# Two turns through the tensor engine moved by one unit in a three-stage attention and expert kernel

## Chip, cores and metric

The kernel runs on 1 core of a Trainium2 chip. The metric is the device time of one execution in microseconds. The kernel before the change took 1273.53 us (median of three runs, 1271.52 to 1274.54).

## What is computed

Two layers over tokens `x` of 4 batches x 512 positions x 256 channels, in float32. Cut to what matters here:

```
x = x + L0_xattn(layernorm(x), ctx, ctx, mask)     # 16 heads of 16 channels, masked softmax
x = x + L0_ffn(layernorm(x))                        # self-attention, then 8 experts, the best one is used
x = x + L1_xattn(layernorm(x), ctx, ctx)            # cross-attention again, no mask
x = x + L1_ffn(layernorm(x))                        # 8 experts, the best one is used

# each attention, per batch and head:
scores = q @ k.T / 4                                # 512 x 512
scores = where(mask == 0, -inf, scores)             # first attention only
out    = softmax(scores) @ v                        # then one projection by W_O for all heads
```

## The kernel before

The program is one sequence of stages on one core: attention `xa0` (cross, masked), attention `sa0` (self), the experts `me0`, attention `xa1` (cross, no mask), the experts `me1`. Every engine has its own instruction list, written out by hand in Python, and semaphores tie them together. What runs first on an engine is the order in which the Python writes it; nothing reorders the work.

An attention stage first projects q, k and v for all batches, splits q and k into bf16 parts and parks them in DRAM. Then `attend_*` does the softmax. Its work is cut so:

- A **batch** has four **groups** of four heads. There are 4 batches, so 16 groups G = 0 to 15 in a stage; g is the group's place in its batch.
- A group has 16 **units** u = 0 to 15: key tile u // 4 (128 keys) and head u % 4.
- Each head is needed twice. Once as scores with queries on partitions, of which VectorE takes the row maximum (`scores`, line 958, and `maximum`, L373 with the mask, L377 without). And once transposed, with keys on partitions, from which ScalarE makes the exponentials (`transposed_scores`, L971, with the mask added by a second product, L975, in `xa0`; `exps`, L885).
- The maxima run 28 units ahead of the exponentials (`LEAD`), since an exponential can only be taken once the maximum of its row is known. The maximum is subtracted inside the product of L971: three extra rows of q hold the negated maximum in three bf16 parts.

How the maxima get there is what the change touches. When the last maximum of a group is taken (unit 3), VectorE cuts the 512 x 4 maxima into three bf16 parts (`split`, four small operations, L1125 to L1131). TensorE **turns** them, in `attend_tensor`'s `maxima(G)`, line 993: four products of 128 x 12 by an identity, so that the result has 12 partitions. They lie in the one spare PSUM bank, `MISC`. ScalarE copies them to SBUF (`attend_scalar`'s `maxima`, L898), and the sync engine sends them by DMA (`shift`, L792) into the extra rows of q, where group G + 1 needs them from its unit 0 on.

The bank `MISC` is shared by all small turns: a user on TensorE first waits until the last one's result was read (`take_misc`). In turn they are the maxima (unit `M_STEP` = 8), the finished output of the group before (`turn`, L1016, unit `TURN_STEP` = 12), in `xa0` the turned mask of the next batch (`turn_mask`, L1005, eight transposes of 128 x 128, at `MASK_STEPS`, group 2 and group 3, unit 9; ScalarE reads each by L904), and the output projection of the batch before (L1025 in group 1, L1036 in groups 2 and 3).

The probabilities times v (`products`, L985) run per key tile, behind the units 5, 9 and 13, and for the last key tile behind unit 1 of the next group. One call is four heads, each with a 32-column stationary operand at its own 32 partitions of the output, in float32. The profile shows eight matrix products for one call.

Six PSUM banks hold the two kinds of scores, three each (`DEEP`), so the transposed scores of unit u wait for the exponentials of unit u - 3 (semaphore `p_exp`), and the scores that TensorE makes in unit u wait for the maximum that was made of the unit three before (`s_max`).

The inner loop of TensorE, cut to what decides the order:

```
for u in range(UNITS):
    transposed_scores(b, g, u, first)
    scores(s, v, ...)
    if at >= 0 and at % HG == 0:          # u = 5, 9, 13
        products(G, g, at // HG)
    if u == M_STEP and not (last and g == NG - 1):
        maxima(G + 1)
    if u == TURN_STEP and not (first and g == 0):
        turn(G - 1)
    if a.masked and not last and (g, u) in MASK_STEPS:
        turn_mask(b + 1, i)
```

ScalarE's loop tests the same two constants: behind the exponentials of unit `M_STEP` stands the copy of the maxima, and behind those of a mask step the copy of the mask.

Of the kernel before, what the change touches and what calls it, by code (L numbers as in the profile page):

```python
# [746 lines left out]
ST, SB = 0, DEEP  # L747
OB = 2 * DEEP
MISC = OB + 1
MASK_STEPS = ((2, 9), (3, 9))  # L750
KEY_TILES = 2
MASK_ROUNDS = T // KEY_TILES
NEXT_STAGE = ((3, 5), (3, 14))
# [1 line left out]
LAST_TURN, LAST_OUT = (5, 2), (3, 4)  # L755
LATE = 2

M_STEP, TURN_STEP = 8, 12
OUT_TURNS = (3, 5)
OUT_TILES = ((2, 3), (2, 4), (3, 3), (3, 4))  # L760

# [114 lines left out]
def attend_scalar(act, a, meanwhile):  # L876
# [24 lines left out]
    def mask_copy(b, i, bank=MISC):  # L901
        act.wait_ge(a.mbT_ps.sem, a.mbT_ps.at(b, i + 1))
        batch = slice(b, b + 1) if type(b) is int else bass.ds(b, 1)
        act.activation(mem.mbT[:, batch, KEY_TILES * i:KEY_TILES * (i + 1), :].rearrange("p b k n -> p (b k n)"),  # L904
                       ps[:, bank, :].bitcast(BF16), ACT.Copy).then_inc(a.mbT_ready.sem, 1)

    def oT_copy(b, c, bank=MISC):
        act.wait_ge(a.oT_ps.sem, a.oT_ps.at(b, c + 1))
        act.activation(mem.oT[:, c, :], ps[:, bank, :], ACT.Copy).then_inc(a.oT_sb.sem, 1)

    def body(b, first, last):
        for g in range(NG):
            G = NG * b + g
            for u in range(UNITS):
# [7 lines left out]
                if last and (g, u) == HALF_TURN:  # L922
                    oT_copy(b, 0, LAST_TURN[0])
                if a.masked and not last and (g, u) in MASK_STEPS:
                    mask_copy(b + 1, MASK_STEPS.index((g, u)))

# [16 lines left out]
def attend_tensor(pe, a, meanwhile):  # L943
# [76 lines left out]
    def turn_out(b, c, bank=MISC):  # L1020
        pe.wait_ge(a.quotient.sem, a.quotient.at(NG * b + (c + 1) * NG // C - 1, QUOTIENT))
        if bank == MISC:
            take_misc()
        for t in range(T):
            ins = pe.transpose(ps[:, bank, t * P:(t + 1) * P], mem.o[:, t, c * P:(c + 1) * P], mem.ident[:, :])  # L1025
        ins.then_inc(a.oT_ps.sem, 1)
        if bank == MISC:
            misc[0] = (a.oT_sb.sem, a.oT_sb.at(b, c + 1))
# [13 lines left out]
    def body(b, first, last):  # L1042
# [4 lines left out]
        for g in range(NG):  # L1047
            G = NG * b + g
            for u in range(UNITS):
# [22 lines left out]
                if last and (g, u) == HALF_TURN:  # L1072
                    turn_out(b, 0, LAST_TURN[0])
                if a.masked and not last and (g, u) in MASK_STEPS:
                    i = MASK_STEPS.index((g, u))
                    if i == 0:
# [1014 lines left out]
```

## Time and profile before

| | |
|---|---|
| median of three runs | 1273.53 us (1271.52 to 1274.54) |
| the profiled execution: its own time | 1274.43 us |
| its span in the profile | 1272.7 us |
| TensorE busy (PE) | 1131.4 us, 89% |
| VectorE busy (DVE) | 838.6 us, 66% |
| ScalarE busy (ACT) | 660.4 us, 52% |
| GpSimd busy (POOL) | 210.9 us, 17% |
| mean granted TensorE clock | 0.949 |

PE is the matrix product, PEld the weight load that goes with it and overlaps other products. In rows of the timeline the first number is the start in us from the start of the span, the second the time covered, then the engine, the line of the kernel and the operation; x4 means that four instructions are merged into the row. A matrix product is shown from its start to a modelled end, and the next one starts before that end: the distance between two starts tells how long TensorE was taken. The attention stages lie at about 60 to 340 us (`xa0`), 395 to 620 us (`sa0`) and 925 to 1165 us (`xa1`).

### The profile page before, as it was taken

What the parts mean: (1) busy time and instruction counts of PE and PEld (TensorE: products, weight loads), DVE (VectorE), ACT (ScalarE), POOL (GpSimd) and SP (SyncE); (2) the same over time, 40 slices, a digit from 0 to 9 for tenths busy, and PEclk for the clock granted to TensorE, in tenths of its full rate; (3) what the DMA queues carried; (4) which work ended last, traced back from release to release, by engine and by line L of the source; (5) the groups of instructions that cost most, each with busy time, mean ns of one, the idle gap of its engine ahead of it and who ended that gap; (6) DMA issues with size and microseconds to landing.
All of it is one profiled execution on the core that took longest, in us unless ns stands there. A gap on an engine that the chain in (4) does not pass through costs nothing. (4 is left out here: it accounts for less than half of the span.)

```text
span 1272.7 us, 17810 instructions
## 1 busy us (share of the span) xinstructions
PE 1131.4 (89%) x5693; PEld 544.0 (43%) x5722; DVE 838.6 (66%) x2112; ACT 660.4 (52%) x1341; POOL 210.9 (17%) x272
## 2 busy tenths in 40 slices
PE   7889999999997999999967999996989999998390
PEld 4423343434453223343364666664523333335370
DVE  5878777777478888888762222223888888876722
ACT  3346666666533677677722333332537767674250
POOL 4310000000143000000202222211520010102154
PEclk9989999999999899999967999998989999999795
DMA  8953321221048433543291140103873323211064
GB/s 265 309 169 93 79 57 28 81 52 26 2 154 291 103 91 90 132 97 93 72 375 33 31 161 28 27 13 102 263 241 91 90 59 89 60 37 57 25 171 144
DMA packets 100706, 139.40 MB, mean 110 GB/s; under 512 B 8452, under 2 KB 82632, under 8 KB 99208
## 3 DMA queue, kind: packets, MB, share of 16 engines
q1 hardware_dynamic: 96536, 128.03, 33.6%
q0 software_dynamic: 4080, 10.23, 2.9%
q8 instruction: 48, 0.79, 0.3%
q14 instruction: 42, 0.34, 0.1%
HBM read 86.30 MB, written 52.17 MB: 109 GB/s over the span
## 5 line engine op out<-in xcount | busy, mean ns | idle before, releaser
L885 ACT ACTIVATE r<-ps 128x512 f32<-128x512 f32 x768 | 427.4, 600 | 211.9 <-PE ps L971 122.1
L377 DVE TENSOR_REDUCE m<-ps 128x1 f32<-128x512 f32 x512 | 320.9, 682 | 45.2 <-PE ps L958 44.9
L971 PE MATMUL ps<-r 99*128 99x512 bf16 x768 | 294.3, 388 | 5.6 <-ACT r L885 5.6
L958 PE MATMUL ps<-r 96*128 96x512 bf16 x720 | 280.9, 393 | 20.5 <-DVE m L377 7.0
L373 DVE CUSTOM_DVE_ANT_0 r<-ps,r 128x512 bf16<-128x512 f32 x256 | 170.2, 690 | 60.2 <-PE ps L958 59.6
L985 PE MATMUL ps<-r 128*32 128x512 f32 x1536 | 204.9, 605 | 4.9 <-ACT r L885 3.3
L971 PEld LDWEIGHTS ps<-r 99*128 99x128 bf16 x768 | 74.4, 98 | 211.7 <-ACT r L885 157.3
L958 PEld LDWEIGHTS ps<-r 96*128 96x128 bf16 x720 | 71.3, 99 | 105.9 <-DVE m L377 24.3
L861 POOL COPY r<-r 128x256 f32<-128x256 f32 x48 | 19.0, 399 | 542.1 <-PE ps L985 542.1
L1660 DVE COPY r<-ps 128x512 f32<-128x512 f32 x46 | 31.8, 691 | 91.9 <-PE ps L1707 91.9
L1707 PE MATMUL ps<-r 128*128 x184 | 87.8, 621 | 2.7 <-issue 0.4
L1619 ACT ACTIVATE r<-ps,cols 128x128 f32<-128x128 f32 x46 | 18.5, 453 | 137.8 <-PE ps L1698 137.8
L657 PE MATMUL ps<-r,w 128*128 128x512 f32 x192 | 88.2, 596 | 0.5 <-issue 0.5
L975 PE MATMUL ps<-r,identb 128*128 128x512 bf16 x227 | 87.5, 386 | 0.0
L1732 PE MATMUL ps<-r 128*128 x368 | 83.3, 380 | 1.1 <-ACT r L1629 1.1
L1671 DVE TENSOR_TENSOR r<-ps,r 128x256 f32<-128x256 f32 x46 | 19.5, 425 | 97.0 <-PE ps L1732 68.8
L1732 PEld LDWEIGHTS ps<-r 128*128 128x128 f32 x368 | 69.9, 190 | 20.1 <-issue 11.9
L589 ACT ACTIVATE r<-ps,cols 128x512 bf16<-128x512 f32 x48 | 32.9, 686 | 86.9 <-PE ps L657 72.7
L985 PEld LDWEIGHTS ps<-r 128*32 128x32 f32 x1536 | 30.3, 108 | 84.0 <-ACT r L885 65.3
L537 POOL TENSOR_TENSOR r<-r 128x512 bf16<-128x512 f32 x48 | 55.0, 1164 | 65.5 <-ACT r L594 65.5
L644 PE MATMUL ps<-w,r 128*128 128x256 f32 x192 | 45.5, 392 | 13.6 <-DMA w<-in_wa 7.4
L1629 ACT ACTIVATE r<-ps,b1c 128x128 f32<-128x128 f32 x184 | 49.9, 382 | 12.9 <-PE ps L1715 12.8
(151 smaller groups left out, 1220.5 us busy)
## 6 DMA issues: line engine op xcount, KB each, us to landing
r<-q_parts SPq DMA_DIRECT2D x48, 384.0 KB, 5.2
r<-k_parts SPq DMA_DIRECT2D x48, 384.0 KB, 6.0
k_parts<-r SPq DMA_DIRECT2D x24, 384.0 KB, 3.3
q_parts<-r SPq DMA_DIRECT2D x24, 384.0 KB, 3.1
r<-in_w SPq DMA_DIRECT2D x16, 512.0 KB, 4.9
r<-in_w SPq DMA_DIRECT2D x8, 1024.0 KB, 14.4
k_parts<-r SPq DMA_DIRECT2D x24, 256.0 KB, 3.3
q_parts<-r SPq DMA_DIRECT2D x24, 256.0 KB, 3.1
```

Source lines behind the costliest of these rows:

```text
L373: ins = dve.tensor_tensor_reduce(mem.junk[bank], mem.ps[:, bank, :], mem.mbS[:, t, :], 1.0, FLOOR, ALU.add, ALU.max, out)
L377: ins = dve.tensor_reduce(out, mem.ps[:, bank, :], AX.X, ALU.max)
L537: pool.tensor_tensor(mem.parts[n][:, 2, :], mem.res[n % 2], mem.parts[n][:, 1, :], ALU.subtract).then_inc(a.lo.sem, 1)
L657: ins = pe.matmul(ps[:, QK_BANK + n, :], a.w[:, 0 if of_query(n) else 1, c, (n % C) * P:(n % C + 1) * P], src[:, c, :], start=(c == 0), st ...
L885: act.activation(mem.probs[:, u // HG, u % HG, :], ps[:, ST + (UNITS * g + u) % DEEP, :], ACT.Exp, scale=SCALE).then_inc(a.p_exp.sem, 1)
L958: pe.matmul(ps[:, led_bank(n), :], mem.qst[g][0:ROWS, h, t * P:(t + 1) * P], mem.kst[g][0:ROWS, h, :], start=True, stop=True).then_inc(a.s ...
L971: ins = pe.matmul(out, mem.kst[g][0:KROWS, h, kt * P:(kt + 1) * P], mem.qst[g][0:KROWS, h, :], start=True, stop=not a.masked)
L975: ins = pe.matmul(out, mem.identb[:, :], mem.mbT[:, batch, kt, :].rearrange("p b n -> p (b n)"), start=False, stop=True)
L985: ins = pe.matmul(ps[h * VW:(h + 1) * VW, OB, :], mem.vg[g % 2][:, kt, h, :], mem.probs[:, kt, h, :], start=(kt == 0), stop=(kt == T - 1))
L1629: ins = act.activation(mem.midT[:, f, :], ps[:, TM[f // 4], (f % 4) * P:(f % 4 + 1) * P], ACT.Relu, bias=mem.b1c[:, bass.ds(e * FT + f, 1)])
L1707: ins = pe.matmul(ps[:, UP[k], :], mem.xT[j % 2][:, c, :], w, start=(c == 0), stop=(c == C - 1))
L1732: ins = pe.matmul(ps[:, DOWN[j % 2], 0:D], mem.midT[:, f, :], w, start=(f == 0), stop=(f == FT - 1))
```

## The change

Two constants are raised by one. Both TensorE and ScalarE (and through a semaphore the DMA of the maxima) follow them.

```diff
-MASK_STEPS = ((2, 9), (3, 9))
+MASK_STEPS = ((2, 10), (3, 10))
...
-M_STEP, TURN_STEP = 8, 12
+M_STEP, TURN_STEP = 9, 12
```

**TensorE, unit 8 and 9 of the first group of `xa0`.** L993 is the turn of the maxima, L971, L975 and L958 are one unit's products, L985 the probabilities times v. Before:

```order
L971 MATMUL ps<-r 128x512 [waits xa0_p_exp]
L975 MATMUL ps<-r,identb 128x512
L958 MATMUL ps<-r 128x512 [waits xa0_s_max]
L993 MATMUL ps<-identb,mparts 12x128 [waits xa0_m_sb,xa0_cut]
L993 MATMUL ps<-identb,mparts 12x128 x3
L971 MATMUL ps<-r 128x512 [waits xa0_p_exp]
L975 MATMUL ps<-r,identb 128x512
L958 MATMUL ps<-r 128x512 [waits xa0_s_max]
L985 MATMUL ps<-r 32x512 [waits xa0_p_exp]
L985 MATMUL ps<-r 32x512 x3
```

Now:

```order
L971 MATMUL ps<-r 128x512 [waits xa0_p_exp]
L975 MATMUL ps<-r,identb 128x512
L958 MATMUL ps<-r 128x512 [waits xa0_s_max]
L971 MATMUL ps<-r 128x512 [waits xa0_p_exp]
L975 MATMUL ps<-r,identb 128x512
L958 MATMUL ps<-r 128x512 [waits xa0_s_max]
L985 MATMUL ps<-r 32x512 [waits xa0_p_exp]
L985 MATMUL ps<-r 32x512 x3
L993 MATMUL ps<-identb,mparts 12x128 [waits xa0_m_sb,xa0_cut]
L993 MATMUL ps<-identb,mparts 12x128 x3
L971 MATMUL ps<-r 128x512 [waits xa0_p_exp]
```

The four narrow products of the maxima (12 columns) stood between two wide ones (128 columns); they now follow the narrow ones of L985 (32 columns). The same happens in all 45 groups that turn maxima inside the loop, 15 in each stage.

**TensorE, units 9 and 10 of the third group of `xa0`,** where the first half of the next batch's mask is turned (L1005). Before:

```order
L985 MATMUL ps<-r 32x512 x3
L1005 MATMUL ps<-identb,r 128x128 [waits xa0_m_sb,xa0_mbS_ready]
L1005 MATMUL ps<-identb,r 128x128 x7
L971 MATMUL ps<-r 128x512 [waits xa0_p_exp]
L975 MATMUL ps<-r,identb 128x512
L958 MATMUL ps<-r 128x512 [waits xa0_s_max]
```

Now:

```order
L985 MATMUL ps<-r 32x512 x3
L993 MATMUL ps<-identb,mparts 12x128 [waits xa0_quotient,xa0_cut]
L993 MATMUL ps<-identb,mparts 12x128 x3
L971 MATMUL ps<-r 128x512 [waits xa0_p_exp]
L975 MATMUL ps<-r,identb 128x512
L958 MATMUL ps<-r 128x512 [waits xa0_s_max]
L1005 MATMUL ps<-identb,r 128x128 [waits xa0_m_sb,xa0_mbS_ready]
L1005 MATMUL ps<-identb,r 128x128 x7
```

Between the turn of the maxima and that of the mask there was a unit, its wide products and the products of a key tile; now there is one unit. The mask turn still waits for `m_sb`, ScalarE's copy of the maxima. This occurs six times.

## Rows read from the trace of the kernel before

**Rows 1.** Stretches `xa0`, `xa1`: busy us (and instructions) of PE, PEld, DVE, ACT, POOL; clock.

```profile
60.00:340.00 280.00, 270.37 (x1495) 104.45 (x1521) 203.55 (x648) 174.02 (x304) 13.53 (x25) 0.98 0.25 70
...
925.00:1165.00 240.00, 227.32 (x1260) 81.42 (x1258) 198.64 (x412) 160.76 (x306) 22.19 (x32) 0.98 0.32 89
```

**Rows 2.** Timeline of PE in `xa1`, units 8 to 10 of group 4.

```profile
1006.26 0.38 PE L958 MATMUL ps<-r 96*128 96x512 bf16 x1
1006.57 0.39 PE L993 MATMUL ps<-identb,mparts 128*12 128x128 bf16 x4
1006.89 0.39 PE L971 MATMUL ps<-r 99*128 99x512 bf16 x1
1007.12 0.38 PE L958 MATMUL ps<-r 96*128 96x512 bf16 x1
1007.43 1.06 PE L985 MATMUL ps<-r 128*32 128x512 f32 x8
1008.43 0.39 PE L971 MATMUL ps<-r 99*128 99x512 bf16 x1
```

**Rows 3.** Timeline of PE: a turn of 128 columns between wide products, in `xa0`.

```profile
105.40 0.38 PE L958 MATMUL ps<-r 96*128 96x512 bf16 x1
105.62 0.60 PE L1016 MATMUL ps<-ident,r 128*128 128x128 f32 x4
106.06 0.38 PE L971 MATMUL ps<-r 99*128 99x512 bf16 x1
```

**Rows 4.** Duration of one instruction of L993, ns: least, median, most.

```profile
L993 PE MATMUL ps<-identb,mparts x192: 215/219/315, 68.5 to 1141.7; 128*12 128x128 bf16 x192
```

**Rows 5.** Timeline of ACT and DVE beside Rows 2.

```profile
1007.03 0.57 ACT L898 ACTIVATE mT<-ps 12x512 bf16<-12x512 bf16 x1
1008.85 0.60 ACT L885 ACTIVATE r<-ps 128x512 f32<-128x512 f32 x1 [0.77 <-PE ps L971]
...
1005.39 1.28 DVE L377 TENSOR_REDUCE m<-ps 128x1 f32<-128x512 f32 x2
1009.07 0.69 DVE L377 TENSOR_REDUCE m<-ps 128x1 f32<-128x512 f32 x1 [0.61 <-PE ps L958]
```

**Rows 6.** Timeline of `xa0`, group 2, which turns the mask: units 8 and 9.

```profile
117.09 0.69 DVE L373 CUSTOM_DVE_ANT_0 r<-ps,r 128x512 bf16<-128x512 f32 x1
117.31 0.39 PE L993 MATMUL ps<-identb,mparts 128*12 128x128 bf16 x4
117.73 0.59 ACT L898 ACTIVATE mT<-ps 12x512 bf16<-12x512 bf16 x1
118.07 0.38 PE L958 MATMUL ps<-r 96*128 96x512 bf16 x1
```

**Rows 7.** Timeline of `sa0`, group 6: units 8 and 9. Then waits of L993 in the program.

```profile
504.75 0.68 DVE L377 TENSOR_REDUCE m<-ps 128x1 f32<-128x512 f32 x1
504.98 0.38 PE L993 MATMUL ps<-identb,mparts 128*12 128x128 bf16 x4 [0.56 <-DVE w L1171]
505.52 0.38 PE L958 MATMUL ps<-r 96*128 96x512 bf16 x1
...
  DVE w L1171: 2.2, 4
```

**Rows 8.** Timeline of `xa1`, group 14: units 8 to 10, and 14 to 0 of group 15.

```profile
1141.22 1.57 ACT L885 ACTIVATE r<-ps 128x512 f32<-128x512 f32 x3 [0.72 <-PE ps L971]
1141.88 0.39 PE L971 MATMUL ps<-r 99*128 99x512 bf16 x1
1142.36 1.07 PE L985 MATMUL ps<-r 128*32 128x512 f32 x8
1143.27 0.72 SPq L792 DMA_DIRECT2D r<-mT  x1
...
1145.92 0.82 PE L971 MATMUL ps<-r 99*128 99x512 bf16 x3
```

**Rows 9.** DMA issues: size and median us from issue to landing.

```profile
cols<-in_cols SPq DMA_DIRECT2D x1, 10.0 KB, 2.0
```

## The prediction

> **What bounds the kernel now.** I read the busy times by stage first. TensorE is busy 270.4 of 280.0 us in `xa0` and 227.3 of 240.0 us in `xa1`; VectorE has 203.6 and 198.6, ScalarE 174.0 and 160.8 [rows 1]. `sa0` looks like `xa1`. So in the attention stages the time is TensorE's, and something that shortens its list shortens the kernel, unless the time saved runs into a wait.
>
> Then the timeline of TensorE around the change, and in it only the distances between starts. Two wide products (128 columns stationary, 512 streamed) follow each other after 0.22 us: L971 at 1006.89, L958 at 1007.12 [rows 2]. From a wide product to the first narrow one it takes 0.31, both into the turn of the maxima (1006.26 to 1006.57) and into the products of a key tile (1007.12 to 1007.43). From the first of the turn to the next wide product it takes 0.32 (1006.57 to 1006.89). One instruction of the turn is shown with 0.219 us [rows 4] and four of them with 0.39, so they start 0.057 us apart, and four need 0.23; the step back to wide costs the rest, 0.09 us. As a control, a turn that is wide itself (L1016) begins 0.22 behind its wide neighbour and its four instructions take 0.44, 0.11 each, with nothing on top [rows 3]. So it isn't turning that costs, but the passage between narrow and wide: 0.09 us in, 0.09 out.
>
> The Trainium skill (TensorEngine Tiling (Array Packing), Key Properties) has a rule for this: changing the tiling mode, not merely the tile, drains the engine. The trace agrees that a passage costs something, 0.09 us. By the same rule nothing is saved if 12 and 32 columns count as different modes; the page doesn't say, and the rivals below price it from rows.
>
> **The change, step by step.**
>
> *The turn itself.* Before, it costs TensorE (0.31 - 0.22) + 0.32 = 0.41 us, two passages included. Now it stands behind products that are narrow already. If narrow to narrow costs no passage, it shares the way in with L985 and leaves only once: the call of L985 takes 1.00 to the next wide product (1007.43 to 1008.43), the turn adds 4 x 0.057 = 0.23. The trace never shows 12 columns behind 32. The bounds are: no passage between them (saving 0.41 - 0.23 = 0.18, with the unrounded starts of these rows 0.19), one passage of 0.09 (saving 0.09), or out and in again (saving 0). I take no passage, because both forms show the same 0.31 on the way in and the same 0.09 on the way out: they look like one mode. **0.19 us a turn**, 45 turns, if nothing waits: 8.4 us at the very most.
>
> *Waits that eat it.* Everything of unit 9 now comes 0.41 us earlier on TensorE, until L985, and the turn is then behind it. Two partners could be late.
>
> VectorE: the scores of unit 9 wait for the maximum of unit 6. TensorE restarts 0.09 us behind VectorE's end (504.75 + 0.68 = 505.43, scores at 505.52) [rows 7]. In group 4 of `xa1` that maximum is the second of two, ends at 1005.39 + 1.28 = 1006.67, and the scores are at 1007.12 [rows 2, 5]: 0.45 of distance, 0.41 asked for, 0.09 needed, so 0.05 is lost and 0.14 left. I find this distance in the first group of a batch (4 and 8 in `sa0`, 4, 8 and 12 in `xa1`): five groups at 0.14. The other plain groups have 0.5 or more.
>
> ScalarE: in the second group of a batch (5, 9, 13 in both stages) the exponentials are later, by the copy of the turned output; there about 0.03 is lost: six groups at 0.16.
>
> `sa0`, groups 6, 7, 10 and 11: VectorE does the residual first (L1171), and TensorE waits for it in front of the turn, 2.2 us in four waits. The scores of unit 9 then wait for VectorE anyway (505.52, 0.09 behind the maximum) [rows 7]. Here the old turn lay inside a wait and was free; the new one lies behind it. **+0.23 each**, four groups.
>
> Group 14 of `sa0` and `xa1` has no scores left, and ScalarE sets the pace. The first of its three exponentials ends at 1141.82, L971 of unit 9 starts at 1141.88 (0.06 behind), so taking the turn away in front of it gains nothing [rows 8]. Behind L985 it costs 0.23, and ScalarE's copy (0.57, in steps of 0.48) then meets the exponentials of unit 10. The turn's last product would start at about 1143.4, the copy 0.25 later (as 117.31 + 0.17 to 117.73) [rows 6], the exponential at about 1144.15, where before it was at 1143.79. **+0.35 each**, two groups.
>
> *ScalarE elsewhere.* The copy falls into an idle stretch: behind the exponential of unit 9, ScalarE waits 0.77 us for L971 of unit 10 [rows 5]. It delays that exponential by about 0.15 against TensorE. The next that needs it is unit 13, three units and more on, and TensorE reaches that later than the exponential ends. Free.
>
> *The mask turn,* six times in `xa0`. Moved from behind narrow products to between wide ones, it changes no passage: L985 still leaves narrow once, eight wide turns cost the same. But it waits for ScalarE's copy of the maxima. From the turn's last start that copy ends 0.25 + 0.59 = 0.84 later and TensorE may go on at 0.90; TensorE itself arrives after 0.15 and a unit of three wide products, 0.66, at 0.81. **0.09 lost**, 0.10 left in five groups. In group 2 the mask's preparation also holds VectorE: the maximum ends at 117.78, the scores stand at 118.07, 0.29 [rows 6], so 0.20 is lost as well: about +0.10. ScalarE's mask copy comes a unit later too, before the turn of unit 12 needs the bank; by the same steps it is out of it 0.04 us in time.
>
> *The DMA of the maxima* is issued some 1.0 us later, and what the sync engine issues behind it too. In group 14 of `xa1`, the tightest, the issue moves from 1143.27 to about 1144.3; unit 0 of group 15, the third of the three, then starts at about 1146.7 (1146.37 before) [rows 8]. 2.4 us are left, where a 10 KB load lands in 2.0 [rows 9]. Free; were it as slow as the 3.1 us that the old distance allows, it would cost 0.7 in each stage's last group.
>
> **The sum.** `xa0`: 9 plain groups x -0.19, 5 x -0.10, +0.10 = -2.1. `sa0`: 5 x -0.19, 2 x -0.14, 3 x -0.16, 4 x +0.23, +0.35 = -0.4. `xa1`: 8 x -0.19, 3 x -0.14, 3 x -0.16, +0.35 = -2.1. Together **-4.6 us**. The profiled execution took 1274.43 (span 1272.7), so 1269.8; it lies 0.9 above the median of the three runs, and on that median the forecast is **1268.9 us**.
>
> **Rivals.**
>
> *One passage remains* between L985 and the turn (a drain because the tile's shape or the number type changes, float32 to bf16). Place: the start of L993 behind the second half of L985. Price: 0.095 per turn, 45 times, 4.3 us: 1273.2. For it: no row shows the pair. Against it: wide float32 to wide bf16 costs nothing (L1016 to L971, 0.11) [rows 3].
>
> *The turn goes out and in again*, as if through the wide mode: L993 would start 0.19 later than I say. Then the saving is nil, and the losses stand alone: -4.6 + 45 x 0.19 = +3.9 us, **1277.4, slower**. It decides from the point where the passage costs more than 0.10 us. For it: 12 and 32 are different column counts. Against it: within L985 the tile changes with every head, and eight instructions fit into 1.00 us.
>
> *No loss anywhere*: the waits I have counted are softer than they look. 45 x 0.19 = 8.4 us, 1265.1. Against it: L993's waits on L1171 are plain in the trace [rows 7].
>
> *The saved time is lost at the next wait* (VectorE or ScalarE bound after all), about -0.5: 1273. Against it: both are idle in front of unit 10, 0.61 and 0.77 us [rows 5], so the groups re-align on TensorE.
>
> **How the numbers follow.** 0.2%, 2.5 us, is about what a measurement of this kernel can tell from no change. Faster by over 0.2%: 0.70 for the forecast and 0.02 for no loss anywhere, 0.72. No change: 0.13 for one passage and 0.07 for the saving lost at the next wait, 0.20. Slower by over 0.2%: 0.06 for out and in again and 0.02 for a DMA that comes late and stalls every group, 0.08. The range reaches down to 1266.4, two thirds of the way to the no-loss case, and up to 1273.6, which holds the one-passage case and the saving lost at the next wait.
>
> **What would show it.** In the profile after: L993 starts about 0.9 us behind the first L985, not 1.0 or more; L971 follows 1.22 to 1.23 behind L985's start where a turn lies between; L993 never waits on L1171; groups of `xa1` last 0.14 to 0.19 us less from turn to turn, group 14 longer; the mask turn shows an idle 0.09 in front of it. Wrong would be: L993 at 1.0 or later behind L985, or shorter distances there and yet the same span.

## The result

The changed kernel takes **1293.47 us** (median of four runs, 1290.26 to 1299.86) where the kernel before took 1274.03 (1271.52 to 1274.58). The ratio is 1.0163, with a 95% interval of 1.0121 to 1.0205: 1.6% slower. The forecast was 1268.9, faster, with a range from 1266.4 to 1273.6. It was wrong in its direction.

The page of the changed kernel: busy times, then two groups of section 5 (busy us, mean ns of one, idle us in front of it and its main releaser).

```profile
span 1290.7 us, 17839 instructions
...
PE 1131.3 (88%) x5722; PEld 547.0 (42%) x5722; DVE 840.9 (65%) x2112; ACT 663.6 (51%) x1341; POOL 210.8 (16%) x272
...
L958 PE MATMUL ps<-r 96*128 96x512 bf16 x720 | 283.5, 396 | 41.8 <-DMA r<-k_parts 24.2
L971 PE MATMUL ps<-r 99*128 99x512 bf16 x768 | 295.7, 390 | 6.1 <-ACT r L885 6.1
```

The first of these groups in the page of the kernel before, and its row among the waits (us in total, times, longest us):

```profile
L958 PE MATMUL ps<-r 96*128 96x512 bf16 x720 | 280.9, 393 | 20.5 <-DVE m L377 7.0
PE ps L958 <- DMA r<-k_parts: 3.4, 8, 0.8
```

TensorE has no more work: it is busy for 1131.3 us, 1131.4 before. VectorE and ScalarE are busy 2 and 3 us longer and stay far from the span, and the mean granted clock is nearly the same (0.947, before 0.949). The span grew by 18.0 us, and one row answers for it: in front of L958, the scores that lead by 28 units, TensorE sat idle for 20.5 us before and now for 41.8, and it is a DMA that L958 waits for, the k stack of a coming group (24.2 us). The profile of before had that wait too, in eight places and with 3.4 us. So I compared where L958 waits, and found one place: unit 4 of a group, where the first scores of the group after next need that group's q and k (its **stacks**, the rows of four heads).

First, though, the turn itself. The timeline of TensorE in `xa1` of the changed kernel, units 9 and 10 of a plain group, answers to [rows 2]:

```profile
1052.67 0.38 PE L971 MATMUL ps<-r 99*128 99x512 bf16 x1
1052.89 0.38 PE L958 MATMUL ps<-r 96*128 96x512 bf16 x1
1053.20 1.07 PE L985 MATMUL ps<-r 128*32 128x512 f32 x8
1054.08 0.39 PE L993 MATMUL ps<-identb,mparts 128*12 128x128 bf16 x4
1054.40 0.39 PE L971 MATMUL ps<-r 99*128 99x512 bf16 x1
```

The turn starts 0.88 us behind L985 and the next wide product 0.32 behind the turn: 1.20 for both, where the forecast said 1.22 to 1.23 and the one-passage rival would give 1.32. The local gain is there, a little larger than forecast.

Now the other end of the chain: the sync engine's timeline in `sa0`, first of the kernel before. L792 sends the turned maxima, L1901 loads a piece of the experts' weights, L334 loads q and k of a coming group.

```profile
451.78 0.72 SPq L792 DMA_DIRECT2D r<-mT  x1
452.56 0.41 SPq L1901 DMA_DIRECT2D r<-in_w  x1
453.02 0.42 SPq L334 DMA_DIRECT2D r<-q_parts  x1
453.48 0.48 SPq L334 DMA_DIRECT2D r<-k_parts  x1
```

And the product that waits for that load, in the timeline of TensorE (unit 4 of the next group):

```profile
459.60 0.38 PE L971 MATMUL ps<-r 99*128 99x512 bf16 x1
460.25 0.39 PE L958 MATMUL ps<-r 96*128 96x512 bf16 x1 [0.27 <-DMA r<-k_parts]
```

The same in the changed kernel, first ScalarE's copy of the maxima and the sync engine:

```profile
454.82 0.59 ACT L898 ACTIVATE mT<-ps 12x512 bf16<-12x512 bf16 x1 [0.66 <-PE ps L993]
...
455.44 0.72 SPq L792 DMA_DIRECT2D r<-mT  x1
456.21 0.41 SPq L1901 DMA_DIRECT2D r<-in_w  x1
456.67 0.42 SPq L334 DMA_DIRECT2D r<-q_parts  x1
457.13 0.48 SPq L334 DMA_DIRECT2D r<-k_parts  x1
```

and TensorE:

```profile
461.73 0.38 PE L971 MATMUL ps<-r 99*128 99x512 bf16 x1
463.70 0.39 PE L958 MATMUL ps<-r 96*128 96x512 bf16 x1 [1.58 <-DMA r<-k_parts]
```

Three things can be read here. First, the loads of the stacks stand behind L792 on the sync engine, which waits for ScalarE's copy. Second, unit 8 of this group began at 450.19 before and at 452.55 now, so the stacks are issued 2.8 us behind it before (453.02) and 4.1 behind it now (456.67): 1.3 us later. Third, in this group they were already too late before: from the issue to the scores 7.2 us pass in the one kernel and 7.0 in the other. Two wide products start 0.22 us apart, so the scores lost 0.43 us there before and 1.75 now.

Summed over the 14 groups of each stage that make scores in unit 4 (from the start of L971 there to the start of L958, less the distance that is usual), this idle time went from 6.0 to 28.0 us: 1.4 to 2.8 in `xa0`, 3.0 to 16.3 in `sa0`, 1.6 to 8.9 in `xa1`. That is +22.0; the span grew by 18.0. The missing 4 would be the turn's gain. The experiments test both halves of this account.

### The profile page after: what moved, and what is told of

Same layout as the page of the kernel before. It is cut to its first block and busy times, and to the rows that moved or that the text cites. A ratio compares the mean times of both kernels' runs of the same rounds, so it can differ in the third digit from the quotient of the medians.

```text
span 1290.7 us, 17839 instructions
## 1 busy us (share of the span) xinstructions
PE 1131.3 (88%) x5722; PEld 547.0 (42%) x5722; DVE 840.9 (65%) x2112; ACT 663.6 (51%) x1341; POOL 210.8 (16%) x272
## 5 line engine op out<-in xcount | busy, mean ns | idle before, releaser
L958 PE MATMUL ps<-r 96*128 96x512 bf16 x720 | 283.5, 396 | 41.8 <-DMA r<-k_parts 24.2
L971 PE MATMUL ps<-r 99*128 99x512 bf16 x768 | 295.7, 390 | 6.1 <-ACT r L885 6.1
L985 PE MATMUL ps<-r 128*32 128x512 f32 x1536 | 206.5, 610 | 4.3 <-ACT r L885 3.3
L971 PEld LDWEIGHTS ps<-r 99*128 99x128 bf16 x768 | 74.7, 99 | 187.5 <-ACT r L885 128.7
L958 PEld LDWEIGHTS ps<-r 96*128 96x128 bf16 x720 | 71.5, 100 | 139.5 <-DMA r<-k_parts 34.4
L975 PE MATMUL ps<-r,identb 128*128 128x512 bf16 x256 | 98.2, 384 | 0.0
L985 PEld LDWEIGHTS ps<-r 128*32 128x32 f32 x1536 | 30.3, 108 | 82.5 <-ACT r L885 65.1
```

The lines of the kernel that those rows point to most:

```text
L958: pe.matmul(ps[:, led_bank(n), :], mem.qst[g][0:ROWS, h, t * P:(t + 1) * P], mem.kst[g][0:ROWS, h, :], start=True, stop=True).then_inc(a.s ...
L971: ins = pe.matmul(out, mem.kst[g][0:KROWS, h, kt * P:(kt + 1) * P], mem.qst[g][0:KROWS, h, :], start=True, stop=not a.masked)
L975: ins = pe.matmul(out, mem.identb[:, :], mem.mbT[:, batch, kt, :].rearrange("p b n -> p (b n)"), start=False, stop=True)
L985: ins = pe.matmul(ps[h * VW:(h + 1) * VW, OB, :], mem.vg[g % 2][:, kt, h, :], mem.probs[:, kt, h, :], start=(kt == 0), stop=(kt == T - 1))
```

## Experiments

Theory A: the late issue of the stacks is the whole loss. Rival B: the moved turn, ScalarE's copy or the mask made it.

**The delay alone.** The kernel before, with nothing moved; the sync engine alone is held back. `G_late` is true for every group but the first.

```diff
         sp.wait_ge(a.m_sb.sem, a.m_sb.at(G, 1))
+        if G_late(G):
+            sp.wait_ge(a.st_ps.sem, a.st_ps.at(G - 1, 11))
         sp.dma_start(mem.qst[g][ROWS:KROWS, :, :], mem.mT[:, :]).then_inc(a.shift[g].sem, 16)
```

> The kernel before, with every engine but the sync engine as it was: the sync engine waits, ahead of sending the maxima, until TensorE has made the transposed scores of unit 10 of the running group, about the moment when ScalarE's copy is ready in the changed kernel (1.2 to 1.3 us later than before). Theory A (the loads of the next q and k stacks, L334, stand behind that wait on the sync engine, and the scores of unit 4 wait for them): slower by about the 22 us by which the idle time before the scores of unit 4 grew, so 1290 to 1300 us, with L958 waiting on k_parts for 25 us or more in all. Rival B (the loss is made on TensorE or ScalarE by the moved turn and copy): no change, 1272 to 1276 us.

Measured: 1297.84 us, ratio 1.0189 (1.0171 to 1.0207). Its waits show the changed kernel's row, at the line shifted by the edit:

```profile
PE ps L964 <- DMA r<-k_parts: 22.1, 19, 2.2
```

where the changed kernel has

```profile
PE ps L958 <- DMA r<-k_parts: 24.2, 19, 2.5
```

In most groups of `sa0` and `xa1` L792 is now issued 2.85 us behind the start of unit 8, where in the plain groups the kernel before has 1.58 and the changed one 2.88. Not one instruction of TensorE, ScalarE or VectorE was moved and the loss is there: the span grew by 21.1 us, and the idle time in front of the scores of unit 4 from 6.0 to 26.0. The median is even 4 us above the changed kernel, which has the turn's gain in it, though the two intervals overlap. The wait on k_parts is 22.1 us, somewhat less than the 25 that were expected. Rival B falls. What this run leaves open is which of the delayed DMAs costs the time, that of the maxima or those of the stacks; the next pair tells them apart.

**The loads taken out from behind the wait.** Both kernels get the same edit: the stacks are loaded three groups ahead instead of two, as soon as the last group that used their buffers is done, and so ahead of the wait for the maxima.

```diff
-            ahead = (b, g + 2) if g < 2 else (b + 1, g - 2)
-            if not (last and g >= 2):
-                if first and g == 2:
+            ahead = (b, g + 3) if g < 1 else (b + 1, g - 1)
+            if first and g == 0:
+                load_stacks(sp, a, 0, 2)
+            if not (last and g >= 1):
+                if first and g == 1:
                     for n in range(QK):
                         sp.wait_ge(a.stored[n].sem, a.stored[n].at(B))
-                if not (first and g < 2):
-                    sp.wait_ge(a.st_ps.sem, a.st_ps.at(G - 1))
+                if not (first and g == 0):
+                    sp.wait_ge(a.st_ps.sem, a.st_ps.at(G))
                 load_stacks(sp, a, *ahead)
```

On the changed kernel:

> The changed kernel, with the loads of the q and k stacks taken out from behind the maxima on the sync engine: they are issued one group further ahead, as soon as the group that used the buffers is done. Theory A: the waits of L958 on k_parts go to nearly nothing (under 2 us in all), and what is left is the saving of the turn: about 1274 - 6 (the old waits before unit 4) - 9 (45 turns x 0.21) + 2 (the losses of some groups) = 1260 us, 1257 to 1266. Rival B: 1285 us or more.

On the kernel before:

> The kernel before with the same edit of the sync engine, and the turns where they were. Theory A: only the 6 us of idle before unit 4 go, about 1268 us (1265 to 1270), so that the moved turns are worth 5 to 8 us against this kernel. Rival B: the same as before, and the changed kernel's loss stays whatever the loads do.

Measured: 1264.60 us with the change (ratio to the kernel before 0.9925, 0.9910 to 0.9939) and 1269.83 without it (0.9968, 0.9955 to 0.9980). The idle time in front of the scores of unit 4 is 0.8 and 0.4 us in all. The kernel with the change still sends its maxima as late as before the edit (L792 stands 2.92 us behind the start of unit 8 in most groups of `sa0`), so it isn't the DMA of the maxima that costs; and no run has a row in which anything waits for it. The sync engine's timeline of that kernel in `sa0`:

```profile
438.27 0.72 SPq L792 DMA_DIRECT2D r<-mT  x1
439.04 0.42 SPq L1903 DMA_DIRECT2D r<-in_w  x1
441.70 0.30 SPq L334 DMA_DIRECT2D r<-q_parts  x1
```

and TensorE at unit 4 of a group there, with nothing in front of the scores:

```profile
444.57 0.38 PE L973 MATMUL ps<-r 99*128 99x512 bf16 x1
444.79 0.38 PE L960 MATMUL ps<-r 96*128 96x512 bf16 x1
```

The stacks issued at 441.70 are needed a group and more later. This pair is also the test of the forecast's own sum, with the late loads out of the way: the change is worth 1264.60 - 1269.83 = **-5.2 us**, against the forecast's -4.6. So one change of two constants costs 19 us in one kernel and gains 5 in another, and the two kernels differ only in when the sync engine loads the stacks.

**Traffic or moment?** Between L792 and the stacks stands the load of weights. In the changed kernel it was put behind the stacks; the wait for the maxima stays ahead of both.

```diff
                 load_stacks(sp, a, *ahead)
+            if pending:
+                meanwhile(sp, *pending.pop())
...
-            if meanwhile is not None:
-                meanwhile(sp, b, g)
+            pending.append((b, g))
```

> The changed kernel; only the loads of the next stage's weights are issued behind the loads of the stacks instead of ahead of them. Theory A: the stacks are issued 0.5 us earlier and land sooner because no 128 to 1024 KB go ahead of them; part of the loss comes back, 1280 to 1288 us. Theory A2 (it is the weights' traffic ahead of them, not the moment of issue, that makes them late): nearly all comes back, below 1275 us. Rival B: no change, 1290 to 1297.

Measured: 1264.80 us (0.9932, 0.9914 to 0.9951). That is the case called A2; the partial recovery to 1280 or more that theory A alone let expect did not come. Here is its sync engine, and then the DMA issues of `sa0` (395 to 620), count, size and median us from issue to landing, of this kernel:

```profile
449.38 0.72 SPq L792 DMA_DIRECT2D r<-mT  x1
450.16 0.41 SPq L334 DMA_DIRECT2D r<-q_parts  x1
450.61 0.47 SPq L334 DMA_DIRECT2D r<-k_parts  x1
451.13 0.48 SPq L1904 DMA_DIRECT2D r<-in_w  x1
```

```profile
r<-in_w SPq DMA_DIRECT2D x15, 512.0 KB, 5.6
r<-q_parts SPq DMA_DIRECT2D x14, 384.0 KB, 4.0
r<-k_parts SPq DMA_DIRECT2D x14, 384.0 KB, 5.1
```

and of the changed kernel:

```profile
r<-in_w SPq DMA_DIRECT2D x14, 512.0 KB, 4.6
r<-q_parts SPq DMA_DIRECT2D x14, 384.0 KB, 5.8
r<-k_parts SPq DMA_DIRECT2D x14, 384.0 KB, 6.6
```

The stacks are issued 0.78 us behind L792 instead of 1.23, and k lands 1.5 us sooner after its issue, now that 512 KB of weights no longer go ahead of it. Together that is 2 us, more than the 1.75 that were lost in the group shown above. So two things had to meet: loads that are needed soon, issued late, and a load that nobody needs yet ahead of them. Taking away either is nearly enough: here 3.3 us of idle time are left in front of unit 4, 1.4 of them in one group of `xa0`. How much of the 2 us each part is worth by itself was not tested, since the edit gives both. The weights take a microsecond longer from issue to landing, and no wait for them shows. It also fits that `xa1` of the changed kernel recovers on its own from its sixth group on (no idle before unit 4 there, with one exception), which was not tested by itself: its weights are 128 KB a group, and the extra 256 KB of biases are loaded beside them in the first four groups only.

The same edit on the kernel before:

> The kernel before, with the loads of weights issued behind the loads of the stacks, as in the fourth kernel. Theory A2 (weights ahead of the stacks cost the landing 1.5 us and the issue 0.5): the 6 us of idle before unit 4 nearly all go, 1268 to 1271 us, as in the third kernel; the moved turns are then worth about 5 us against it. Without A2: 1272 to 1275.

Measured: 1270.09 us (0.9980, 0.9963 to 0.9997), as expected with A2, though the interval reaches close to 1. In `sa0` its stacks land 3.8 and 4.8 us after their issue, 6.1 and 6.8 in the kernel before, and the idle time in front of the scores of unit 4 is 0.4 us. The moved turns are worth 5.3 us between these two kernels (1264.80 against 1270.09, not run side by side), as the first pair says.

**The two constants apart.**

> The kernel before with only the turns of the mask one unit later; the turns of the maxima stay at unit 8, so the sync engine is not held back. Theory A: within 2 us of before (1272 to 1276), since no load moves but that of the next mask, and a wide turn between wide products costs what it did. If the mask's part made the loss: 1280 us or more.

Measured: 1273.52 us (0.9998, 0.9982 to 1.0014). The later turns of the mask cost nothing that can be measured.

> The kernel before with only the turns of the maxima one unit later; the mask is turned in the same unit, directly behind them, and there waits some 0.8 us for ScalarE's copy, six times. Theory A: the whole loss is here, 1290 to 1300 us, up to 4 us above the changed kernel for those six waits. If the mask's part made the loss: about 1265 to 1272 us.

Measured: 1295.46 us (1.0191, 1.0158 to 1.0224). The whole loss comes with `M_STEP`. Its trace has the expected wait of the mask's turn for ScalarE's copy, six times, 4.3 us in all; whether that makes the run slower than the changed kernel can't be told, since the intervals overlap.

**The turn placed per group.** The distances from one unit 8 to the next show in which groups the later turn costs more than it saves (see below). In those it was left at unit 8. The edit stands on the changed kernel with its loads taken out from behind the wait.

```diff
-MASK_STEPS = ((2, 10), (3, 10))
+MASK_STEPS = ((2, 9), (3, 10))
...
+def m_step(a, g, first, last):
+    if a.masked:
+        early = g == 2 and not last
+    else:
+        early = (last and g == 2) or (a.self_block and g >= 2 and not first)
+    return M_STEP - 1 if early else M_STEP
...
-                if u == M_STEP and not (last and g == NG - 1):
+                if u == m_step(a, g, first, last) and not (last and g == NG - 1):
```

> The second kernel (changed turns, stacks loaded a group further ahead), but in the groups in which the later turn costs more than it saves the turn stays at unit 8: group 2 of each batch of xa0 (with its mask turn at unit 9), groups 2 and 3 of the later batches of sa0, and group 14 of sa0 and xa1. From the distances of the second and third kernels' units 8 to 8: 0.23 + 2 x 0.03 in xa0, 4 x 0.18 + 0.33 in sa0, 0.33 in xa1, so 1.7 us less than the second kernel's 1264.6: 1263, range 1261 to 1265. If the groups re-align elsewhere and the local losses cost nothing: 1264.6 as before.

Measured: 1263.62 us (0.9929, 0.9907 to 0.9951), 9 us below the kernel before. Against the kernel that it stands on (1264.60, ratio 0.9925) no gain can be told from the times: the ranges overlap (1260.52 to 1265.46 and 1262.86 to 1265.39), and against the kernel before, which ran again beside each, the two ratios are the same within 0.0004. In the traces the groups do what was expected: added up over unit 8 to unit 8 they are 0.3, 1.2 and 0.4 us shorter in the three stages, 1.8 in all where 1.7 was expected.

## Why the prediction was wrong

**What bounds the kernel:** right. The time is TensorE's, and the time went where TensorE idles.

**The passage between narrow and wide:** right. No passage lies between 32 and 12 columns. The trace shows L993 0.88 us behind L985; with one passage it would have been 0.97 or more. By the Trainium skill (TensorEngine Tiling (Array Packing), Key Properties) a change of the tiling mode drains the engine and a change of the tile alone does not. That is in line with the 0.88 us if 12 and 32 columns count as one mode, which the page does not say.

**The waits that eat it:** right in kind and nearly in size, as the pair of kernels without late loads shows (change of the distance from unit 8 to unit 8, us):

```
                                     forecast   measured
xa0 plain group                       -0.19      -0.22
xa0 mask turn, group 3 of a batch     -0.10      -0.05
xa0 mask turn, group 2 of batch 0     +0.10      +0.24
sa0, xa1 plain group                  -0.19      -0.15 to -0.22, one -0.29
sa0, xa1 first, second of a batch  -0.14, -0.16  -0.17 to -0.18
sa0 groups 6, 7, 10, 11               +0.23      +0.18
group 14 of sa0 and xa1               +0.35      +0.34, +0.33
sum of 45 groups                      -4.6       -4.9
```

By stage the forecast was -2.1, -0.4 and -2.1, and the pair shows -1.8, -0.7 and -2.4. The mask turns were dearer than forecast. In the third group of every batch that turns a mask it starts 0.38 to 0.39 us behind the scores (119.91 to 120.29 below, TensorE's timeline in the changed kernel), not 0.22 + 0.09; in the fourth it starts 0.30 behind them, as forecast. And in all six groups the turn of the finished output in unit 12 (L1016) now starts 0.27 us behind its scores (121.83 to 122.10), where before it started 0.22 behind them. That points to ScalarE's copy of the mask, which the forecast had out of the bank 0.04 us in time; it ends at 121.96. So in the third group of the later batches, forecast with -0.10, the gain is used up (+0.03).

```profile
119.14 0.39 PE L993 MATMUL ps<-identb,mparts 128*12 128x128 bf16 x4
...
119.91 0.38 PE L958 MATMUL ps<-r 96*128 96x512 bf16 x1
120.29 0.61 PE L1005 MATMUL ps<-identb,r 128*128 128x128 bf16 x8
...
121.83 0.38 PE L958 MATMUL ps<-r 96*128 96x512 bf16 x1
122.10 0.63 PE L1016 MATMUL ps<-ident,r 128*128 128x128 f32 x4
```

**The step that failed** is the one on the DMA of the maxima: "is issued some 1.0 us later, and what the sync engine issues behind it too", which the prediction then puts down as "Free". It named the queue and then followed only the transfer of the maxima to its reader. What is issued behind it are the q and k stacks, and their reader, the scores of unit 4, was never looked up. The delay is 1.3 us in the plain groups of `sa0` and `xa1`, and the trace of before had the sign of it: L958 already waited for k_parts in eight places. Where it waited, nothing was left to take up a delay; in the other groups of `sa0` little was, since 13 of its 14 groups now wait 0.35 to 1.65 us longer in unit 4, as do four of `xa1` (1.4 to 2.4) and one of `xa0` (1.5). The rival with a late DMA had a chance of 0.02, and the only late DMA that the prediction prices is that of the maxima. The two measured terms, the groups' gain and the wait for the stacks, give 1274.0 - 4.9 + 22.0 = 1291 us, 2 us from what was measured; the forecast had the first of them and not the second.

## What to carry to other kernels

When a step is moved, follow its result to every engine that waits for it, and there read the list of what stands behind that wait, not only what the wait is for; each of those has a reader with a slack of its own. A wait on a DMA that shows up in a profile with a few tenths of a microsecond in several places (here 3.4 us in eight) is a load without slack, and its neighbours may have little: here 1.3 us of delay cost 22 us in some 18 groups. And on an engine that issues its DMAs in the order of its list, loads that somebody needs soon go ahead of waits and of loads that nobody needs yet: here the one alone was worth 4 us to the kernel before and the other alone 2.5, and either turned the changed kernel from 19 us above it into 9 below.

## What the hardware showed

In the changed kernel a turn of 12 columns starts 0.41 us behind the last start of a group of four products of 32 columns (a wide product starts 0.52 behind it), and the four instructions of the turn still start 0.06 us apart. Of the 0.11 between the two, 0.09 is the passage read from [rows 2]; the remaining 0.02 is as long as the four heads' starts are apart, as if the turn, which writes the first partitions alone, had only to wait for the first head. That is read from starts, and was not tested by itself.

Stacks of 384 KB each (q and k), issued behind 512 KB of weights in `sa0`, land 5.8 and 6.6 us after their issue in the changed kernel; without the weights ahead, 4.0 and 5.1.
